# Reordering the first two slots of an eight-graph GNN and attention pipeline: mask tiles, row copies, value loads, VectorE's queue, and the last gathers ahead of a scatter

## The chip, the core and the metric

One core of a Trainium2 chip runs the whole program. The metric is the device time of one execution in microseconds; lower is better. The engines are TensorE (PE; its weight loads are PEld), VectorE (DVE), ScalarE (ACT), GpSimd (POOL) and the DMA queues, two of which are filled by SyncE (SP) and by ACT, and one by POOL.

## What is computed

The input is `x` (8 graphs, 1024 nodes, 128 features, float32) and `adj` (8 x 1024 x 1024, int32, about 8 ones in a row). Two layers follow each other, each `x = x + layer(relu(layernorm(x)))`:

```python
# layer 0: for each node, the elementwise maximum over its first 25 neighbours
agg = max(h[idx[:25]]);  out = relu(concat([h, agg]) @ W + b)
# layer 1: masked attention (8 heads of 16), then a feed-forward block
allowed = (adj > 0) | (adj.T > 0) | eye
ctx = softmax(where(allowed, q @ k.T * scale, -inf)) @ v
x = layernorm(x + ctx @ Wo.T + bo)
x = layernorm(x + relu(x @ W1.T + b1) @ W2.T + b2)
```

## The kernel before

The graphs go through a software pipeline of **slots** `s`. In slot `s` the attention of graph `g = s` runs in 32 steps `n` (a step is 8 matmuls and 16 mask matmuls of scores on PE, two exponentials on ACT, and 8 context matmuls on PE, one step behind). Around them, spread over fixed steps, run the closing work of graph `p = s-1` (output projection, feed-forward), the front of `f = s+1` (layer 0's linear part, projections, value rows, masks), the pooling of `r = s+2` and the neighbour lists of `l = s+3`. Every engine's queue is an order written out by hand, and engines meet through semaphores. An instruction that waits holds up all that stands behind it in its queue.

What the change and the prediction touch:

- **Neighbour lists** (DVE). `list_tile(l, t)` makes keys of an adjacency tile that SP loaded, and takes chunk maxima; `merge_pair` merges two tiles; `find_crowded`, `crowded_tiles`, `make_lists` and `list_ranks` finish the lists of a graph. PE helps at two steps (`RANK_AT`): it turns `full` at slot 1's step 11 for graph 3, and counts ranks at step 12 (`rank_counts`), after `make_lists` has written `abovesum`. `rank_counts` and the turn of `full` share PSUM bank 2 with `context_rows`, so they wait for `context` on DVE, which frees it.
- **Scatter and load of lists** (POOL). `scatter_lists(r)` writes the lists sorted by length to DRAM with eight indirect DMAs; `load_lists(r)` reads them back when all eight have landed; the gathers of graph `r` wait for that.
- **Gathers** (POOL). `gather_tile(f, t)` issues one indirect DMA for each neighbour level: for graphs from 2 on some 20 for tile 0, and down to 5 for tile 7. Each is held back until a step of the scores is done (`paced`, tables `PACE_2`, `PACE_3`), and the first of a tile until the tile two before it is pooled. `pool_tile(f, t)` on DVE takes the maxima, and `send(f, t)` on POOL scatters its result to DRAM. When all eight have landed SP loads them back as `ag` (`load_pooled`), and PE turns `ag` at step 20 of graph `f`'s slot `s = f-1`.
- **Order of POOL for graph 2.** Gathers of tile 6, `send(2, 4)`, `scatter_lists(3)`, `beta2(1)` (an elementwise add on 128 x 1024), gathers of tile 7, `send(2, 5)`, `load_lists(3)`, `send(2, 6)`, `send(2, 7)`, gathers of graph 3.
- **Feed-forward of graph 0, second half, in slot 1.** PE needs `add_input(0, 1)` of DVE before it can turn the sum at step 17.
- **Slot 2's step 3.** PE turns both halves of graph 1's context there, and the second half needs `context(1, 3)`, which stands behind `pool_tile(3, 3)` in DVE's queue (`middle`).
- **Masks** (ACT). `mask_tile` converts an adjacency tile and then issues the load of the next one into the same buffer `adj_m`, at the steps of `MASK_AT`.
- **Row copies** (ACT). `first_norm(l, t)` normalizes the rows of graph `l` in place at the steps of `H_AT_1` for graph 3; SP then stores them.
- **Value loads** (SP). `turn_values(f, hg)` moves the value rows of four heads with seven DMAs; the first contexts of a slot wait for `turn_values(f, 0)`. For graph 1 it stands behind `load_list_tile(3, 5)`.

Of the kernel before, what the change touches and what calls it, by code (L numbers as in the profile page):

```python
# [42 lines left out]
PACE_1 = [(4, 3, 0, 8), (9, 3, 0, 10), (11, 3, 0, 12), (13, 3, 0, 14), (14, 3, 0, 15), (15, 3, 0, 16), (16, 3, 0, 16), (16, 3, 0, 16)]  # L43
PACE_2 = [(25, 3, 0, 31), (32, 3, 1, 35), (35, 3, 1, 38), (38, 3, 1, 41), (41, 3, 1, 43), (43, 3, 1, 45), (45, 3, 2, 47), (49, 3, 0, 50)]
PACE_3 = [(19, 4, 0, 24), (24, 4, 0, 26), (27, 4, 0, 29), (29, 3, 0, 31), (32, 3, 0, 34), (35, 3, 1, 37), (38, 3, 0, 39), (43, 3, 2, 45)]
EARLY_FIRSTS = 28
SCATTER_PACE = {2: 20, 3: 47}
SCATTER_LATE = 40
# [16 lines left out]
H_AT = {17: (0, 2), 19: (2, 4), 21: (4, 5), 22: (5, 8)}  # L65
H_AT_1 = {22: (0, 4), 23: (4, 8)}

CTXT_AT, EARLY_CTXT_AT = [{3}, {3}], {20}
# [9 lines left out]
PROJ_BANK = dict(pair for pairs in PROJ_AT.values() for pair in pairs)  # L78
VALUE_BANK = (1, 2)
MASK_AT = {4: 0, 7: 1, 11: 2, 12: 3, 15: 4, 16: 5, 18: 6, 21: 7}  # L80
AGGS = 4
# [97 lines left out]
def program(nc, x, adj, L0_W, L0_b, Wqkv, bqkv, Wo, bo, ln1_g, ln1_b, W1, b1, W2, b2, ln2_g, ln2_b, out):  # L179
# [6 lines left out]
    with ctx:  # L186
# [256 lines left out]
        with nc.Block() as block:  # L443

            @block.sync
            def _(sp):
# [92 lines left out]
                def first_slot():  # L539
                    load_shift(0, 0)  # L540
                    turn_values(0, 1)
                    load_list_tile(2, 2)
                    load_list_tile(2, 3)
                    store_h_rows(2)
                    load_list_tile(2, 4)
                    load_h(1)
                    load_list_tile(2, 5)
                    load_x1_half(1, 0)
                    load_list_tile(2, 6)
                    load_x1_half(1, 1)  # L550
                    load_list_tile(2, 7)
                    load_x(3)
                    load_list_tile(3, 0)
                    load_list_tile(3, 1)
                    load_pooled(1)
                    load_shift(0, 1)
                    store_h_rows(3)
                    for t in range(2, 6):
                        load_list_tile(3, t)
                    turn_values(1, 0)  # L560

                prologue()
# [55 lines left out]
            def _(pool):  # L618
# [33 lines left out]

                def scatter_lists(r):
                    pool.wait_ge(s_ranks, 2 * (r + 1))
                    k = r % 2
                    for t in range(T):
                        pool.wait_ge(s_scores, scatter_paced(r, t))
# [58 lines left out]
                for f in range(B):  # L716
# [6 lines left out]
                    for t in range(T):  # L723
# [3 lines left out]
                        if f and t >= 2:  # L727
                            send(f, t - 2)
                        if t == T - 2 and f >= AHEAD:
                            if f + 1 < B:  # L730
                                scatter_lists(f + 1)
                            beta2(f - 1)
                    if f == 1:
                        send(f, T - 2)
                        send(f, T - 1)
                        scatter_lists(f + 1)
                        beta2(f - 1)
                    if f:
                        if f + 1 < B:
# [4 lines left out]
                            load_lists(f + 1)  # L744
                        if f >= AHEAD:
                            send(f, T - 2)
# [6 lines left out]
            def _(dve):  # L753
# [486 lines left out]
                def second_slot():  # L1240
# [12 lines left out]
                    find_crowded()  # L1253
                    merge_pair(6)
                    pool_tile(2, 3)
                    context(1, 0)
                    crowded_tiles(3)
                    make_lists(3)
                    pool_tile(2, 4)
                    list_ranks(3)  # L1260
                    list_tile(4, 0)
                    add_input(0, 0)
                    first_norm(4)
                    finish(0, 0)
                    pool_tile(2, 5)
                    list_tile(4, 1)
                    merge_pair(0)
                    wide_maxima(1, 1)
                    pool_tile(2, 6)
                    add_input(0, 1)  # L1270
                    list_tile(4, 2)
                    finish(0, 1)
                    context(1, 1)
                    pool_tile(2, 7)
                    list_tile(4, 3)
                    merge_pair(2)
# [55 lines left out]
                for s in range(1, B + 1):  # L1332
# [15 lines left out]
                    if live(r):  # L1348
                        pool_tile(r, 0)
                        pool_tile(r, 1)  # L1350
                    if live(g):
# [16 lines left out]
                    if live(f):  # L1368
                        largest(f, 3)
                        products(f)  # L1370
                        flag(f)
                    if live(r):
                        pool_tile(r, 2)
# [5 lines left out]
            def _(act):  # L1379
# [118 lines left out]
                for s in range(-3, B + 1):  # L1498
                    g, p, f, r, l = s, s - 1, s + 1, s + 2, s + 3
                    for n in range(STEPS):  # L1500
# [19 lines left out]
                        if s == -2 and n == 10:  # L1520
                            for kt, bank in NEAR_0:
                                bar(0, kt, bank, 0, s_near_counts, s_near_ready)
                        if f and live(f) and n in MASK_AT:
                            mask_tile(f, MASK_AT[n])
                        if s == 0 and n in (7, 8):
                            for t in range((n - 7) * TH, (n - 6) * TH):
                                first_norm(2, t)
                        if live(l) and l not in (0, 2):
                            for t in range(*(H_AT if l > 4 else H_AT_1).get(n, (0, 0))):
                                first_norm(l, t)  # L1530
# [385 lines left out]
```

## Time and profile before

| what | value |
|---|---|
| median of three runs | 1263.07 us (1261.59 to 1265.48) |
| the profiled execution's own time | 1266.34 us |
| its span, first to last instruction | 1263.8 us |
| PE busy, share of the span | 1053.1 us, 83% |
| ACT busy | 806.7 us, 64% |
| DVE busy | 798.5 us, 63% |
| POOL busy | 737.2 us, 58% |
| mean granted share of the TensorE clock | 0.952 |

The profile is one execution. Busy times are those of the engines, without their sequencers' waits and register work; a gap of POOL of about 0.3 us between two indirect DMAs is its issue. In a timeline the bracket tells how long the engine had been idle before the instruction, and what ended that. Engine totals say little here, since each slot has its own limits: the views by slot and by engine do.

### The profile page before, as it was taken

The numbers are of one execution on the slowest core, as the hardware profiler recorded it, in microseconds if no ns is written. First come the engines' busy times: TensorE is split into PE (matmuls) and PEld (weight loads), VectorE is DVE, ScalarE is ACT, GpSimd is POOL, SyncE is SP. The second block draws the span as 40 slices with busy tenths as digits, with TensorE's granted clock in tenths as the row PEclk, the third lists the DMA queues.
The fourth block names the chain that finished last, engine by engine and source line by source line (L and its number), as shares of the span: only waits on it lengthen the run. The fifth ranks groups of instructions, "written<-read, shape, count | busy, mean of one in ns | idle before, by whom it ended". The sixth has DMA issues, their size and how long they took to land.

```text
span 1263.8 us, 29316 instructions
## 1 busy us (share of the span) xinstructions
PE 1053.1 (83%) x11014; PEld 407.3 (32%) x11014; DVE 798.5 (63%) x3052; ACT 806.7 (64%) x1031; POOL 737.2 (58%) x743
## 2 busy tenths in 40 slices
PE   0125687788994989999999999999999999999874
PEld 0112331233331424343434333433343334333222
DVE  7856777668778476977697768776363534122323
ACT  1130256667763767788768876887778767875541
POOL 4776677557777777777777767777777620000000
PEclk9986788999997999999999999999999999999996
DMA  6743337616443535563557354623452331000000
GB/s 189 254 127 104 94 115 192 214 52 152 135 152 110 158 88 164 160 163 87 162 165 161 87 162 149 175 83 98 129 118 67 93 103 51 18 4 10 10 9 9
DMA packets 104372, 144.33 MB, mean 114 GB/s; under 512 B 18104, under 2 KB 76992, under 8 KB 104192
## 3 DMA queue, kind: packets, MB, share of 16 engines
q1 hardware_dynamic: 68352, 62.67, 16.1%
q0 software_dynamic: 22816, 44.61, 15.6%
q10 hardware_dynamic: 13024, 34.75, 8.2%
q8 instruction: 101, 1.65, 0.5%
q14 instruction: 79, 0.65, 0.2%
HBM read 124.65 MB, written 12.85 MB: 109 GB/s over the span
## 4 chain that ended last, share of the span: by engine, by line
PE 60%; ACT 13%; DVE 9%; POOL 6%; DMA 6%; issue 5%; ACTq 0%; SPq 0%; DVEq 0%; POOLq 0%
PE sc L1658 19%; PE cb L1678 12%; ACT probs L1443 11%; PE sc L1662 6%; PE m L1735 4%; PE m L1743 3%; POOL nb_low L707 3%; DMA adj_m<-in_adj_dram 3%; POOL nb_low L685 2%; PE m L1564 2%; PE sc L1700 2%; PE m L1587 2%; DMA nb_low<-h_rows,lsorted 1%; ACT m L1459 1%; PE m L1592 1%
## 5 line engine op out<-in xcount | busy, mean ns | idle before, releaser
L1443 ACT ACTIVATE probs<-sc 128x1024 f32<-128x1024 f32 x512 | 496.5, 1023 | 237.7 <-PE sc L1662 230.4
L685 POOL DMA_INDIRECT nb_low<-h_rows,lsorted x474 | 470.3, 992 | 175.4 <-issue 127.5
L1678 PE MATMUL cb<-probs,va 128*17 128x512 f32 x2048 | 272.9, 605 | 4.9 <-issue 3.9
L1658 PE MATMUL sc<-q_near,k_g 32*128 32x512 f32 x1024 | 150.4, 658 | 24.3 <-ACT probs L1443 20.5
L1658 PE MATMUL sc<-q_far,k_g 32*128 32x512 f32 x1024 | 148.7, 648 | 22.3 <-ACT probs L1443 21.2
L998 DVE TENSOR_REDUCE agg<-nb_low 128x128 f32<-128x1024 f32 (+10 forms) x58 | 96.3, 1661 | 59.4 <-DMA nb_low<-h_rows,lsorted 32.6
L1662 PE MATMUL sc<-barred,negident 32*32 32x512 bf16 x4096 | 113.2, 389 | 1.5 <-issue 1.4
L817 DVE MAX8 cand<-keys 128x8 f16<-128x128 f16 x512 | 105.3, 278 | 2.2
L707 POOL DMA_INDIRECT nb_low<-h_rows,first_lists x80 | 81.6, 1020 | 41.6 <-issue 22.9
L1662 PEld LDWEIGHTS sc<-barred,negident 32*32 32x32 bf16 x4096 | 35.4, 88 | 201.0 <-issue 201.0
L1459 ACT ACTIVATE m<-adj_m 128x1024 bf16<-128x1024 int32 x64 | 67.8, 1059 | 44.6 <-DMA adj_m<-in_adj_dram 44.6
L813 DVE SCALAR_TENSOR_TENSOR keys<-adj_t,prio 128x1024 f16<-128x1024 int32 x64 | 78.6, 1228 | 9.2 <-DVEq L1005 6.6
L1435 ACT ACTIVATE barred<-m 128x512 bf16<-128x512 f32 x128 | 72.9, 609 | 10.3 <-PE m L1592 9.4
L665 POOL DMA_INDIRECT pooled_rows<-agg,lsorted x56 | 59.4, 1060 | 27.3 <-issue 14.0
L658 POOL DMA_INDIRECT neighbour_lists<-lst,rank_i x48 | 49.4, 1028 | 31.7 <-DVE rank_i L893 18.3
L1735 PE MATMUL m<-turned,w1T 128*128 128x512 f32 x128 | 65.5, 636 | 1.0 <-ACT turned L1427 1.0
L1658 PEld LDWEIGHTS sc<-q_near,k_g 32*128 32x128 f32 x1024 | 41.1, 187 | 74.4 <-ACT probs L1443 48.3
L1658 PEld LDWEIGHTS sc<-q_far,k_g 32*128 32x128 f32 x1024 | 40.6, 184 | 70.9 <-ACT probs L1443 49.9
L1743 PE MATMUL m<-wide_tiles,w2T 128*128 128x512 f32 x128 | 63.1, 617 | 0.0
L1678 PEld LDWEIGHTS cb<-probs,va 128*17 128x17 f32 x2048 | 34.1, 95 | 64.0 <-issue 63.3
L685 POOL DMA_INDIRECT nb_high<-h_rows,lsorted x46 | 46.3, 1006 | 14.0 <-issue 12.5
L1475 ACT ACTIVATE wide_tiles<-m,b1c 128x512 f32<-128x512 f32 x64 | 44.0, 687 | 15.3 <-PE m L1735 13.8
(183 smaller groups left out, 1448.9 us busy)
## 6 DMA issues: line engine op xcount, KB each, us to landing
adj_t<-in_adj_dram SPq DMA_DIRECT2D x64, 512.0 KB
adj_m<-in_adj_dram ACTq DMA_DIRECT2D x64, 512.0 KB
nb_low<-h_rows,lsorted POOLq DMA_INDIRECT x474
xh<-in_x_dram SPq DMA_DIRECT2D x8, 512.0 KB
h_rows<-xh SPq DMA_DIRECT2D x8, 512.0 KB
hl<-h_rows SPq DMA_DIRECT2D x8, 512.0 KB
x<-in_x_dram SPq DMA_DIRECT2D x16, 256.0 KB
out_dram<-h2T SPq DMA_DIRECT2D x16, 256.0 KB
```

Source lines behind the costliest of these rows:

```text
L685: pool.indirect_dma_start(out=dst, out_offset=None, in_=h_rows[0:(f + 1) * (N + 1), :], in_offset=bass.IndirectOffsetOnAxis(ap=lsorted[:, ...
L707: pool.indirect_dma_start(out=first_slots(t)[:, k, :], out_offset=None, in_=h_rows[0:(f + 1) * (N + 1), :], in_offset=bass.IndirectOffsetO ...
L813: nc.vector.scalar_tensor_tensor(out=keys[:, t, :], in0=adj_t[:, t % 2, :], scalar=0.0, in1=prio[:, :], op0=ALU.not_equal, op1=ALU.mult).t ...
L817: ch.step(nc.vector.max(cand[:, t, 8 * c:8 * c + 8], keys[:, t, c * CW:(c + 1) * CW]))
L998: ch.link(nc.vector.tensor_reduce(a, first.rearrange("p k c -> p c k"), AX.X, ALU.max))
L1443: nc.scalar.activation(probs[:, i % 2, 2 * pair:2 * pair + 2, :], sc[:, 2 * pair:2 * pair + 2, :], ACT.Exp, scale=SCALE).then_inc(s_probs, 1)
L1459: nc.scalar.activation(m1[:, t, :], adj_m[:, :], ACT.Relu).then_inc(s_m1_ready, 1)
L1658: nc.tensor.matmul(sc[:, a, :], k[part, :], q[part, :], start=True, stop=False)
L1662: last = nc.tensor.matmul(sc[c * SPAN:(c + 1) * SPAN, a, :], negident[b, b], barred[b, kt, qh * HALF:(qh + 1) * HALF], start=False, stop=True)
L1678: last = nc.tensor.matmul(cb[a * SPAN:a * SPAN + VW, :], va[:, u % 2, a, kt, :], probs[:, i % 2, a, :], start=(kt == 0), stop=(kt == T - 1))
L1735: nc.tensor.matmul(m[:, bank, :], w1T[:, k * P:(k + 1) * P], turned[:, half * HALF:(half + 1) * HALF], start=True, stop=True).then_inc(s_h ...
L1743: last = nc.tensor.matmul(m[:, half, :], w2T[:, k, :], hid[:, k, :], start=(k == 0), stop=(k == FC - 1))
```

## The change

- `MASK_AT_0` gives the mask tiles of graph 1 (in slot 0) other steps: 4, 6, 10, 12, 14, 16, 19, 21 in place of 4, 7, 11, 12, 15, 16, 18, 21.
- `H_AT_3` moves the row copies of graph 3 from steps 22 and 23 to 24 and 25.
- On SP, `turn_values(1, 0)` goes ahead of `load_list_tile(3, 5)`.
- DVE's `second_slot` gets another order: `context(1, 0)` ahead of `pool_tile(2, 3)`; after `list_ranks(3)` come `add_input(0, 0)`, `pool_tile(2, 5)`, `list_tile(4, 0)`, `finish(0, 0)`, `first_norm(4)`, `pool_tile(2, 6)`, `wide_maxima(1, 1)`, `add_input(0, 1)`, `list_tile(4, 1)`, `finish(0, 1)`, `context(1, 1)`, `pool_tile(2, 7)`, and only then `merge_pair(0)` and the further list tiles. `pool_tile(3, 1)` moves behind `flag(2)`.
- On POOL, graph 2's gathers of tile 7 and `send(2, 5)` go ahead of the scatter of graph 3's lists. The scatter is cut in two: four tiles, `send(2, 6)`, `send(2, 7)`, four tiles, then `beta2(1)` and `load_lists(3)`.
- `PACE_2`, `PACE_3` and `SCATTER_PACE` get other steps for these parts.

```diff
--- before.py
+++ after.py
@@ -41,10 +41,10 @@
 
 PACE = [(15, 3, 0, 21), (21, 3, 1, 24), (25, 3, 0, 28), (28, 3, 2, 31), (32, 3, 0, 34), (35, 3, 1, 37), (38, 3, 0, 39), (43, 3, 2, 45)]
 PACE_1 = [(4, 3, 0, 8), (9, 3, 0, 10), (11, 3, 0, 12), (13, 3, 0, 14), (14, 3, 0, 15), (15, 3, 0, 16), (16, 3, 0, 16), (16, 3, 0, 16)]
-PACE_2 = [(25, 3, 0, 31), (32, 3, 1, 35), (35, 3, 1, 38), (38, 3, 1, 41), (41, 3, 1, 43), (43, 3, 1, 45), (45, 3, 2, 47), (49, 3, 0, 50)]
-PACE_3 = [(19, 4, 0, 24), (24, 4, 0, 26), (27, 4, 0, 29), (29, 3, 0, 31), (32, 3, 0, 34), (35, 3, 1, 37), (38, 3, 0, 39), (43, 3, 2, 45)]
+PACE_2 = [(25, 3, 0, 31), (32, 3, 1, 35), (35, 3, 1, 38), (38, 3, 1, 41), (41, 3, 1, 43), (43, 3, 1, 45), (45, 3, 2, 47), (47, 3, 1, 48)]
+PACE_3 = [(20, 4, 0, 25), (25, 4, 1, 27), (27, 4, 0, 29), (29, 3, 0, 31), (32, 3, 0, 34), (35, 3, 1, 37), (38, 3, 0, 39), (43, 3, 2, 45)]
 EARLY_FIRSTS = 28
-SCATTER_PACE = {2: 20, 3: 47}
+SCATTER_PACE = {2: 20, 3: 48}
 SCATTER_LATE = 40
 
 
@@ -64,6 +64,7 @@
 NEAR_AT_1 = {17: [(0, 2), (1, 0)], 20: [(2, 2)], 21: [(3, 2)], 23: [(4, 2)], 24: [(5, 2)], 25: [(6, 2)], 31: [(7, 2)]}
 H_AT = {17: (0, 2), 19: (2, 4), 21: (4, 5), 22: (5, 8)}
 H_AT_1 = {22: (0, 4), 23: (4, 8)}
+H_AT_3 = {24: (0, 4), 25: (4, 8)}
 
 CTXT_AT, EARLY_CTXT_AT = [{3}, {3}], {20}
 OUTPROJ_AT, EARLY_OUTPROJ_AT = [{4}, {5}], {21}
@@ -77,6 +78,7 @@
 PROJ_AT_1 = {28: [(0, 0), (1, 1)], 29: [(2, 2), (3, 0)]}
 PROJ_BANK = dict(pair for pairs in PROJ_AT.values() for pair in pairs)
 VALUE_BANK = (1, 2)
+MASK_AT_0 = {4: 0, 6: 1, 10: 2, 12: 3, 14: 4, 16: 5, 19: 6, 21: 7}
 MASK_AT = {4: 0, 7: 1, 11: 2, 12: 3, 15: 4, 16: 5, 18: 6, 21: 7}
 AGGS = 4
 
@@ -555,9 +557,10 @@
                     load_pooled(1)
                     load_shift(0, 1)
                     store_h_rows(3)
-                    for t in range(2, 6):
+                    for t in range(2, 5):
                         load_list_tile(3, t)
                     turn_values(1, 0)
+                    load_list_tile(3, 5)
 
                 prologue()
                 first_slot()
@@ -650,10 +653,10 @@
                     k = r % 2
                     pool.dma_start(lsorted[:, k, :, :], rows_of(lists[k])).then_inc(s_lists_in, 16)
 
-                def scatter_lists(r):
+                def scatter_lists(r, tiles=(0, T)):
                     pool.wait_ge(s_ranks, 2 * (r + 1))
                     k = r % 2
-                    for t in range(T):
+                    for t in range(*tiles):
                         pool.wait_ge(s_scores, scatter_paced(r, t))
                         pool.indirect_dma_start(out=lists[k][:, :], out_offset=bass.IndirectOffsetOnAxis(ap=rank_i[:, t:t + 1], axis=0),
                                                 in_=lst[:, t, :], in_offset=None).then_inc(s_lists_out, 16)
@@ -726,7 +729,7 @@
                         gather_tile(f, t)
                         if f and t >= 2:
                             send(f, t - 2)
-                        if t == T - 2 and f >= AHEAD:
+                        if t == T - 2 and f > AHEAD:
                             if f + 1 < B:
                                 scatter_lists(f + 1)
                             beta2(f - 1)
@@ -735,6 +738,12 @@
                         send(f, T - 1)
                         scatter_lists(f + 1)
                         beta2(f - 1)
+                    if f == AHEAD:
+                        scatter_lists(f + 1, (0, TH))
+                        send(f, T - 2)
+                        send(f, T - 1)
+                        scatter_lists(f + 1, (TH, T))
+                        beta2(f - 1)
                     if f:
                         if f + 1 < B:
                             if f == 1:
@@ -742,7 +751,7 @@
                             for k in range(AGGS) if f > 1 else ():
                                 pool.wait_ge(s_pooled_out[k], 16 * T // AGGS * (f - 1))
                             load_lists(f + 1)
-                        if f >= AHEAD:
+                        if f > AHEAD:
                             send(f, T - 2)
                             send(f, T - 1)
                 beta2(B - 1)
@@ -1252,26 +1261,26 @@
                     list_tile(3, 7)
                     find_crowded()
                     merge_pair(6)
+                    context(1, 0)
                     pool_tile(2, 3)
-                    context(1, 0)
                     crowded_tiles(3)
                     make_lists(3)
                     pool_tile(2, 4)
                     list_ranks(3)
+                    add_input(0, 0)
+                    pool_tile(2, 5)
                     list_tile(4, 0)
-                    add_input(0, 0)
+                    finish(0, 0)
                     first_norm(4)
-                    finish(0, 0)
-                    pool_tile(2, 5)
+                    pool_tile(2, 6)
+                    wide_maxima(1, 1)
+                    add_input(0, 1)
                     list_tile(4, 1)
-                    merge_pair(0)
-                    wide_maxima(1, 1)
-                    pool_tile(2, 6)
-                    add_input(0, 1)
-                    list_tile(4, 2)
                     finish(0, 1)
                     context(1, 1)
                     pool_tile(2, 7)
+                    merge_pair(0)
+                    list_tile(4, 2)
                     list_tile(4, 3)
                     merge_pair(2)
 
@@ -1347,7 +1356,8 @@
                         low_levels(r)
                     if live(r):
                         pool_tile(r, 0)
-                        pool_tile(r, 1)
+                        if s > 1:
+                            pool_tile(r, 1)
                     if live(g):
                         context(g, 2)
                     if s == B - 1:
@@ -1369,6 +1379,8 @@
                         largest(f, 3)
                         products(f)
                         flag(f)
+                    if s == 1:
+                        pool_tile(r, 1)
                     if live(r):
                         pool_tile(r, 2)
                     if live(l):
@@ -1520,13 +1532,14 @@
                         if s == -2 and n == 10:
                             for kt, bank in NEAR_0:
                                 bar(0, kt, bank, 0, s_near_counts, s_near_ready)
-                        if f and live(f) and n in MASK_AT:
-                            mask_tile(f, MASK_AT[n])
+                        masks = MASK_AT_0 if f == 1 else MASK_AT
+                        if f and live(f) and n in masks:
+                            mask_tile(f, masks[n])
                         if s == 0 and n in (7, 8):
                             for t in range((n - 7) * TH, (n - 6) * TH):
                                 first_norm(2, t)
                         if live(l) and l not in (0, 2):
-                            for t in range(*(H_AT if l > 4 else H_AT_1).get(n, (0, 0))):
+                            for t in range(*(H_AT if l > 4 else H_AT_3 if l == 3 else H_AT_1).get(n, (0, 0))):
                                 first_norm(l, t)
                         if live(f):
                             if n in (18, 19) if f else n in (3, 4):
```

## Rows read from the trace of the kernel before

**Rows 1.** Windows of slots 0 to 2: length, then busy us of PE, PEld, DVE, ACT, POOL.

```profile
166.40:303.40 137.00, 113.33 (x1382) 41.56 (x1386) 100.50 (x420) 94.92 (x124) 89.25 (x87) 0.95 0.50 143
303.40:466.00 162.60, 130.76 (x1355) 49.77 (x1347) 119.21 (x435) 100.26 (x129) 124.26 (x122) 0.92 0.47 132
466.00:592.50 126.50, 124.00 (x1360) 47.87 (x1363) 95.75 (x363) 100.19 (x129) 96.00 (x96) 1.00 0.51 143
```

**Rows 2.** Timeline of ACT, slot 0: start, us, instruction [idle before <-releaser].

```profile
221.18 1.06 ACT L1459 ACTIVATE m<-adj_m 128x1024 bf16<-128x1024 int32 x1 [3.87 <-DMA adj_m<-in_adj_dram]
...
238.88 1.06 ACT L1459 ACTIVATE m<-adj_m 128x1024 bf16<-128x1024 int32 x1 [1.95 <-DMA adj_m<-in_adj_dram]
...
264.56 1.65 ACT L1467 ACTIVATE xh<-xh,nw 128x128 f32<-128x128 f32 x4 [3.68 <-DVE nw L781]
```

**Rows 3.** Timeline of PE, slot 1.

```profile
310.49 1.91 PE L1678 MATMUL cb<-probs,va 128*17 128x512 f32 x8 [3.88 <-issue]
...
354.84 0.27 PE L1839 MATMUL m<-identf,full 128*1 128x128 f32 x1 [1.59 <-DVE ctxn L1017]
...
390.84 1.11 PE L1751 MATMUL m<-identf,turned 128*128 128x128 f32 x4 [9.52 <-DVE turned L1037]
```

**Rows 4.** Timeline of POOL, slots 0 and 1.

```profile
258.25 1.17 POOL L658 DMA_INDIRECT neighbour_lists<-lst,rank_i  x1 [11.15 <-DVE rank_i L893]
...
366.66 0.94 POOL L685 DMA_INDIRECT nb_low<-h_rows,lsorted  x1 [0.30 <-PE sc L1662]
...
378.03 1.23 POOL L658 DMA_INDIRECT neighbour_lists<-lst,rank_i  x1 [0.30 <-issue]
...
389.08 2.35 POOL L714 TENSOR_TENSOR x<-x,bias_rows 128x1024 f32<-128x1024 f32 x1
...
404.09 1.88 POOL L665 DMA_INDIRECT pooled_rows<-agg,lsorted  x1 [1.93 <-DMA lsorted<-neighbour_lists]
...
406.28 1.00 POOL L685 DMA_INDIRECT nb_low<-h_rows,lsorted  x1 [0.31 <-issue]
```

**Rows 5.** Chain of work of slot 1, in order of time: start, us, what.

```profile
356.58 3.03 DMA nb_low<-h_rows,lsorted
...
399.70 4.19 DMA lsorted<-neighbour_lists
...
404.09 3.15 DMA pooled_rows<-agg,lsorted
...
407.39 4.23 DMA ag<-pooled_rows
```

**Rows 6.** Timeline of DVE, slot 1 and the start of slot 2.

```profile
363.07 1.22 DVE L813 SCALAR_TENSOR_TENSOR keys<-adj_t,prio 128x1024 f16<-128x1024 int32 x1
...
366.54 1.64 DVE L758 BATCH_NORM_STATS2 st<-xh 128x6 f32<-128x128 f32 x8
...
371.54 0.88 DVE L758 BATCH_NORM_STATS2 st<-m 128x6 f32<-128x128 f32 x4
...
378.42 1.73 DVE L998 TENSOR_REDUCE agg<-nb_low 128x128 f32<-128x896 f32 x1
...
388.11 1.46 DVE L998 TENSOR_REDUCE agg<-nb_low 128x128 f32<-128x768 f32 x1 [2.25 <-issue]
...
390.04 0.75 DVE L1037 SCALAR_TENSOR_TENSOR turned<-m,b2c,turned 128x512 f32<-128x512 f32 x1 [0.46 <-DVEq L1005]
...
394.12 0.87 DVE L758 BATCH_NORM_STATS2 st<-m 128x6 f32<-128x128 f32 x4
...
402.17 1.29 DVE L998 TENSOR_REDUCE agg<-nb_low 128x128 f32<-128x640 f32 x1 [0.28 <-issue]
...
471.19 2.16 DVE L998 TENSOR_REDUCE agg<-nb_low 128x128 f32<-128x1152 f32 x1 [2.75 <-DMA nb_low<-h_rows,lsorted]
...
474.10 0.42 DVE L1017 TENSOR_TENSOR ctxn<-m,rden 128x256 f32<-128x256 f32 x1
```

**Rows 7.** Timeline of PE, fourth step of slot 2.

```profile
477.64 1.09 PE L1564 MATMUL m<-identf,ctxn 128*128 128x128 f32 x8
```

## The prediction

> **What bounds the kernel now.** I first read the windows by slot [rows 1]. Slot 2 takes 126.5 us with PE busy for 124.0 at the full clock: a settled slot is PE's. Slots 0 and 1 take 137.0 and 162.6 us, so there are some 10 and 36 us above a settled slot, and all that this change can give lies there. The same rows show the second bound. POOL has 96 instructions in slot 2, nearly all indirect DMAs of 0.94 us with a gap of 0.30 [rows 1, 4]: 96 x 1.25 = 120 of 126.5 us. In slot 1 it is 122 instructions, 122 x 1.25 = 152 of 162.6. So GpSimd, which the page lists at 58%, has 6 us of room in a settled slot, and whatever makes its queue late stays late for slots.
>
> Next I read the timelines of the waits. In slot 0 ACT waits twice for the one mask buffer, 3.87 and 1.95 us, and once, 3.68 us, for the rows of graph 3 [rows 2]. In slot 1 PE waits 3.88 us at the first contexts, 1.59 us for `context(1, 0)`, and 9.52 us for `add_input(0, 1)` [rows 3]. At step 20 it waits again: lists load, send, load of `ag` in a chain of 4.19, 3.15 and 4.23 us [rows 5].
>
> **The change part by part.**
>
> *Masks.* With two steps between a load and its use both mask waits can go: up to 3.87 + 1.95 = 5.8 us. *Row copies*: up to 3.68 us, less what the four copies (1.65 us, [rows 2]) add to each of two later steps. I take 2. *Value loads*: seven DMAs start earlier and without an adjacency tile of 512 KB ahead of them; the 3.88 us go. The tile's own load is then some seven issues later, and `list_tile(3, 5)` stands behind two other large parts of DVE's queue, so that cover hides it. *context(1, 0)*: 1.59 us.
>
> None of this reaches the end by itself, since in slot 1 the next thing late is the pooling of graph 2, and that is POOL's. How much earlier does POOL get? Its graph 2 work begins with the scatter, which waited 11.15 us for the ranks [rows 4], a product of DVE and PE. The mask waits lie ahead of it, so POOL gains between 0 and 5.8 us; DVE is busy for 100.5 of 137 us there [rows 1] and would be next. I take 2.5.
>
> *DVE's second slot.* Before, tile 5 of graph 2 was pooled late enough (378.42, no wait) [rows 6]. Its last gather is issued at 366.66 [rows 4], and a gather lands 3.0 us after its issue [rows 5], so the data is there at 369.7, or 367.2 with POOL 2.5 earlier. In the new order only `add_input(0, 0)` stands between `list_ranks(3)` (its end is 363.07, with the shift 360.6) and this pooling: DVE now idles some 6 us, which is as much as it saves by moving a list tile and a merge back. From 367.2 on the queue runs without waits [rows 6]:
>
> - `pool_tile(2, 5)` 1.73 + 0.46 = 2.2
> - `list_tile(4, 0)`: 366.54 - 363.07 = 3.5 with `add_input` in it, less its 0.75 = 2.7
> - `finish(0, 0)`: 378.42 - 371.54 = 6.9
> - `first_norm(4)`: 371.54 - 366.54 = 5.0
> - `pool_tile(2, 6)` 1.46 + 0.46 = 1.9, and the value load of `wide_maxima`, at most the 2.25 seen before 388.11
>
> Sum 21.0: `add_input(0, 1)` starts at 388.2 in place of 390.04. PE's long wait is hardly shorter: 1.8 us gained. Then `add_input` and a list tile 3.5, `finish(0, 1)` and `context(1, 1)` 402.17 - 394.12 = 8.1, `pool_tile(2, 7)` 1.3: it is done at 401.1, where it was 403.5.
>
> *POOL's order.* Before, scatter (378.03 to 389.08, 11.05 us for eight) and `beta2` (2.35) ran while DVE was on its way to tile 7, and the lists' load landed just before the last send; the first gather of graph 3 came at 406.28 [rows 4]. Now half of the scatter, `beta2` and the load stand behind `send(2, 7)`, which waits for 401.1. POOL has nothing to do while it waits there. After it: send 1.3, four scatters 5.5, `beta2` 2.5, load until landed 4.2 [rows 5], and 0.2: the first gather of graph 3 comes at 401.2 + 13.7 = 414.9, which is **8.6 us later** than before. With POOL's gain at its bounds (0 and 5.8) it is 11.1 or 5.3 later.
>
> The Trainium skill ("DMA: Bandwidth & Descriptors", section "Anatomy of one DMA - SWDGE (gpsimd) path") has 2.0 us plus the bytes over 436 GB/s for a DMA that GpSimd issues, 2.3 us for the 128 KB of lists. The row shows 4.19, and the measurement decides; by the page's figure the delay would be 1.9 us less and the forecast 1267.
>
> *Where it lands.* In the rest of slot 1 the new place of `pool_tile(3, 1)` frees `context(1, 2)` from a late gather, and `ag` comes at 401.2 + 3.15 + 4.23, some 3 us earlier than before, if no list tile's load gets ahead of it. Slot 2 can thus start up to 4 us early. But at slot 2's step 3 PE needs `context(1, 3)`, which stands behind `pool_tile(3, 3)`, and that one already waited 2.75 us for its gathers and started at 471.19 [rows 6]. Between there and 406.28 POOL ran back to back, so it moves by the full 8.6: to 479.8. The context was done at 474.5, 3.3 us after 471.19 [rows 6]; now 483.1. PE wanted the first half at 477.64 and the second about 0.5 later [rows 7], so there was a slack of 3.6, and PE is 8.6 - 3.6 = 5.0 us later than before. After such an idle stretch eight context matmuls take 1.91 us [rows 3], and slot 1's clock is 0.92 against 1.00 in slot 2 [rows 1]; that, and the next pooled tiles that are 8.6 late too, add between 0 and 3.6 (then nothing of the slack is left). I take 1. From there slots are PE's again and don't give it back; POOL's 6 us of room per slot only restores its slack.
>
> **Sum.** +6.0 us. The profiled execution took 1266.34, so 1272.3 in its terms; it lies 3.3 above the median of the runs, so the median goes from 1263.07 to 1269.1. With the bounds of the delay: 5.3 - 3.6 = +1.7, and 11.1 - 3.6 + 1.5 = +9: own range 1264.8 to 1272.
>
> **The rivals.**
>
> *A. The delay doesn't reach PE.* If the first gather of graph 3 starts before 406.28 + 3.6 = 409.9, slot 2 keeps its early start and the kernel is 4 us faster, 1259. It needs `pool_tile(2, 7)` done by 396.1, 5 us ahead of my sum, so POOL's gain at its bound and a shorter queue on DVE. For: the list tile and the merge are out of the way. Against: the 34 us behind tile 5 are plain durations. 0.15.
>
> *B. Most waits come out in full*: 5.8 + 3.7 + 3.9 + 1.6 = 15.0 us, 1248. For: each is on PE's or ACT's own queue. Against: POOL fills 152 us of slot 1. The Trainium skill ("Perfetto Trace Analysis", section "Optimization Strategies") speaks for this one: when TensorE idles for another engine, speed up what blocks it. 0.07.
>
> *C. The two cancel*: the delay is 3 to 6 us, most of it slack, and the time stays within 0.3%. 0.20.
>
> **Chances.** Forecast 0.58, A 0.15, B 0.07, C 0.20. A change within 0.3%, 3.8 us, can't be told from none. Faster 0.22 (A, B), same 0.20, slower 0.58. The range leaves B out and takes A's time in with 2 us about it, and 1 us above my own range: 1257 to 1273.
>
> **What the next profile would show.** Right: ACT's two mask waits and the wait before the first contexts are gone; DVE idle before `pool_tile(2, 5)`, about 6 us; PE's wait at step 17 still over 8 us; POOL idle about 10 us ahead of `send(2, 7)`; the first gather of graph 3 at 413 to 417; slot 2's fourth step with a PE wait of 8 to 9 us for `context(1, 3)`. Wrong: if that first gather comes by 410, A holds; if slot 2 has no such wait though the gather is late, DVE's slack was larger than rows 7 tell; if tile 5 lands before 364, all times of DVE after it move, and the forecast with them.

## The result and the profile after

The kernel after takes **1274.66 us** (median of four runs, 1273.75 to 1275.99) where the kernel before takes 1262.33 (four runs beside it). The ratio is 1.0097, with a 95% interval of 1.0081 to 1.0113: **12.3 us slower**. The sign was forecast; the size was put at +6.0, and 1274.66 lies above the range (1257 to 1273). The profiled execution of the kernel after took 1275.99 us, 9.65 more than the profiled one of before (1266.34). The first lies 1.3 us above the median of its kernel's runs and the second 4.0, so the traces show a smaller difference than the medians do.

The starts of the steps on PE, read from the two timelines and subtracted, say where the time went. Slot 0 starts 2.2 us earlier, slot 1 3.6 earlier and slot 2 0.2 earlier; the two steps behind the turn of graph 1's context in slot 2 start 10.1 and 11.1 *later*, and from there the distance stays between 11.4 and 10.2 to the end. So all of the loss that the traces show is one stall. The windows of slots 0 to 2 (columns as in [rows 1]) show it in the third row, with 10.9 us more than before for the same work:

```profile
164.20:299.50 135.30, 109.79 (x1382) 41.27 (x1386) 100.23 (x417) 94.55 (x124) 88.13 (x84) 0.94 0.49 142
299.50:465.60 166.10, 132.41 (x1354) 49.74 (x1348) 113.91 (x428) 101.03 (x129) 114.00 (x114) 0.92 0.46 128
465.60:603.00 137.40, 125.47 (x1340) 48.26 (x1340) 97.21 (x372) 100.20 (x128) 105.38 (x105) 0.96 0.48 136
```

The timeline of PE has the stall itself, the turn of the second half of graph 1's context in slot 2's fourth step, and ahead of it the wait at step 17 of slot 1:

```profile
389.58 1.12 PE L1764 MATMUL m<-identf,turned 128*128 128x128 f32 x4 [9.29 <-DVE turned L1046]
...
487.63 1.12 PE L1577 MATMUL m<-identf,ctxn 128*128 128x128 f32 x4 [9.55 <-DVE ctxn L1026]
```

The timeline of DVE: tile 5 of graph 2, the second half's `add_input`, tile 7, and then tiles 2 and 3 of graph 3 with the context that PE waits for:

```profile
367.67 1.71 DVE L1007 TENSOR_REDUCE agg<-nb_low 128x128 f32<-128x896 f32 x1 [5.08 <-DMA nb_low<-h_rows,lsorted]
...
388.77 0.75 DVE L1046 SCALAR_TENSOR_TENSOR turned<-m,b2c,turned 128x512 f32<-128x512 f32 x1 [1.97 <-issue]
...
400.02 1.26 DVE L1007 TENSOR_REDUCE agg<-nb_low 128x128 f32<-128x640 f32 x1 [0.28 <-issue]
...
470.50 2.39 DVE L1007 TENSOR_REDUCE agg<-nb_low 128x128 f32<-128x1280 f32 x1 [7.71 <-DMA nb_low<-h_rows,lsorted]
484.33 2.08 DVE L1007 TENSOR_REDUCE agg<-nb_low 128x128 f32<-128x1152 f32 x1 [5.75 <-DMA nb_low<-h_rows,lsorted]
487.15 0.42 DVE L1026 TENSOR_TENSOR ctxn<-m,rden 128x256 f32<-128x256 f32 x1
```

And the timeline of POOL: the first scatter in slot 0, and then from the last send of graph 2 to the first gather of graph 3:

```profile
257.50 1.17 POOL L661 DMA_INDIRECT neighbour_lists<-lst,rank_i  x1 [10.61 <-DVE rank_i L902]
...
401.92 0.97 POOL L668 DMA_INDIRECT pooled_rows<-agg,lsorted  x1 [11.84 <-DVEq L1016]
403.19 0.97 POOL L661 DMA_INDIRECT neighbour_lists<-lst,rank_i  x1 [0.30 <-issue]
...
408.97 2.35 POOL L717 TENSOR_TENSOR x<-x,bias_rows 128x1024 f32<-128x1024 f32 x1
413.87 0.93 POOL L654 DMA_DIRECT2D lsorted<-neighbour_lists  x1 [2.55 <-issue]
419.15 1.01 POOL L688 DMA_INDIRECT nb_low<-h_rows,lsorted  x1 [4.34 <-issue]
```

Read from the last list back to the first, this is the whole delay. The first gather of graph 3 starts at 419.15 against 406.28 [rows 4], 12.9 us later. Tile 3 is pooled at 484.33 against 471.19 [rows 6], 13.1 later. PE had 3.6 us of slack there and waits 9.55.

### The profile page after: what moved, and what is told of

It is laid out like the page before. It is cut to its first block, busy times and chain, and to the rows that moved or that the text cites. A ratio compares the mean times of both kernels' runs of the same rounds, so it can differ in the third digit from the quotient of the medians.

```text
span 1274.1 us, 29318 instructions
## 1 busy us (share of the span) xinstructions
PE 1054.0 (83%) x11014; PEld 408.3 (32%) x11014; DVE 795.0 (62%) x3052; ACT 807.8 (63%) x1031; POOL 731.9 (57%) x743
## 4 chain that ended last, share of the span: by engine, by line
PE 59%; DVE 12%; ACT 12%; DMA 6%; POOL 5%; issue 5%; DVEq 0%; ACTq 0%; POOLq 0%; SPq 0%
PE sc L1671 18%; PE cb L1691 11%; ACT probs L1455 10%; PE sc L1675 6%; PE m L1748 4%; PE m L1756 3%; POOL nb_low L710 3%; DMA nb_low<-h_rows,lsorted 3%; PE m L1577 3%; POOL nb_low L688 2%; DVE agg L1007 2%; PE m L1600 2%; PE sc L1713 2%; PE m L1605 1%; PE m L1778 1%
```

## The experiments

All ratios are to the kernel before on the same chip, with 95% intervals; before took 1263.1 to 1263.2 us beside e1 to e9, and 1262.55 beside e14 to e17. "Landed" is the start of `pool_tile(3, 3)`, which waits for tile 3's gathers (before: 471.19; after: 484.33), and "PE's wait" is the one at slot 2's fourth step. The landed times hold to some 3 us only: e1 and e8, whose code is the same up to there, start slot 1 4.0 and 6.9 us earlier than before does. A wait is read within one execution and is free of that.

| run | what | us | ratio | landed | PE's wait |
|---|---|---|---|---|---|
| e1 | after, old order on POOL | 1265.88 | 1.0032 (1.0015 to 1.0050) | 475.6 | 6.69 |
| e2 | before, new order and pace tables of POOL | 1275.18 | 1.0090 (1.0066 to 1.0114) | 489.2 | 18.13, elsewhere |
| e3 | after, both sends last | 1268.71 | 1.0052 (1.0026 to 1.0078) | 476.2 | 6.63 |
| e7 | after, scatter and `beta2` in the gap | 1268.91 | 1.0046 (1.0030 to 1.0062) | 479.0 | 7.65 |
| e8 | e1 with old `PACE_3` | 1266.73 | 1.0033 (1.0016 to 1.0050) | 472.9 | 7.04 |
| e9 | e8, loads held | 1264.36 | 1.0016 (0.9996 to 1.0036) | 473.7 | 3.47 |
| e4 | before, slot 0's edits | 1261.32 | 0.9988 (0.9973 to 1.0002) | 465.7 | under 1 |
| e5 | before, DVE's orders | 1270.40 | 1.0052 (1.0029 to 1.0074) | 477.5 | 6.60 |
| e14 | before, `pool_tile(3, 1)` late | 1266.11 | 1.0030 (1.0012 to 1.0047) | 476.7 | 7.53 |
| e15 | after, `pool_tile(3, 1)` back | 1275.56 | 1.0112 (1.0089 to 1.0136) | 483.2 | 15.31, elsewhere |
| e16 | e9, `pool_tile(3, 1)` earlier | 1262.12 | 0.9998 (0.9983 to 1.0013) | 469.7 | under 1 |
| e17 | e4 with e16's last two edits | 1261.06 | 0.9991 (0.9976 to 1.0007) | 471.3 | 1.12 |

### Is it the order on POOL?

**e1** is the kernel after with before's queue on POOL; **e2** is the kernel before with after's queue on POOL. Cut of e1's edit, against the kernel after:

```diff
-                    if f == AHEAD:
-                        scatter_lists(f + 1, (0, TH))
-                        send(f, T - 2)
-                        send(f, T - 1)
-                        scatter_lists(f + 1, (TH, T))
-                        beta2(f - 1)
```

> The changed kernel with GpSimd's old order for graph 2 (whole scatter and beta2 ahead of the gathers of tile 7, lists' load ahead of the last two sends, old PACE_2 and SCATTER_PACE). Theory (GpSimd's lists come late): the first gather of graph 3 is back at 403 to 407 us and the wait at slot 2's step 3 is gone, 1258 to 1262 us. Rival (VectorE's new order, with pool_tile(2,5) and pool_tile(3,1) elsewhere, makes slot 2 late): still 1270 to 1275.

> The kernel before with GpSimd's new order and the new pace tables alone. Theory: pool_tile(2,7) ends near 403.5, so the first gather of graph 3 comes at 419 to 422 and the time is 1275 to 1278 us. Rival (VectorE's order): within 3 us of before, 1260 to 1265.

e2 alone costs 12 us, as much as the whole change, and lies in its range; its first gather of graph 3 came later still than expected (424.50). But taking the same edit out of the whole (e1) gives back only some 8 of them: e1 is still 1.0032, where the theory had a gain over before. In e1 the first gather of graph 3 is early (403.79), and yet PE waits 6.69 us at the same place. Something else in the change makes the same data late.

**e3** and **e7** keep the new order otherwise and only move what stands behind the sends: in e3 scatter, `beta2` and load all go ahead of `send(2, 6)`, in e7 the load alone stays behind. Cut of e3's edit, against the kernel after (its two sends now follow the load):

```diff
-                        scatter_lists(f + 1, (0, TH))
+                        scatter_lists(f + 1)
+                        beta2(f - 1)
                         send(f, T - 2)
                         send(f, T - 1)
-                        scatter_lists(f + 1, (TH, T))
-                        beta2(f - 1)
```

> The changed kernel, but after the gathers of tile 7 GpSimd issues all eight scatters, beta2 and the lists' load, and the two sends last. Theory: it has the early gathers without the wait ahead of the lists; first gather of graph 3 at 403 to 407, time 1258 to 1262. Rival: 1270 to 1275.

> The changed kernel with all eight scatters and beta2 ahead of the two sends, the lists' load behind them. Only the load (some 5.3 us from issue to landing) stands behind the wait for pool_tile(2,7). Theory: first gather of graph 3 near 408.5, 2 us later than before, inside VectorE's slack at slot 2's step 3: 1260 to 1263. If there is no slack and each us of delay costs one: 1264 to 1266. Rival (VectorE's order): 1270 to 1275.

Both missed in the same way as e1. The first gather came at 404.22 and 409.24, 14.9 and 9.9 us earlier than after, yet the time fell by about 6 us, not 12. They size the queue behind `send(2, 7)`: with nothing there (e3) the first gather follows 1.3 us after it, with the load alone (e7) 5.4 us (403.88 to 409.24), with all (after) 17.2. What keeps them above before looks like what e1 has: big loads of SP at 466.67 and 468.38, and a last gather of tile 3 that takes 6.88 and 6.42 us.

### What else makes tile 3 late?

Windows of 468 to 476 us, of the kernel before and then of e1 (the last three columns are PE's granted clock, the DMA engines' share and GB/s):

```profile
468.00:476.00 8.00, 7.92 (x96) 2.91 (x93) 3.64 (x8) 6.40 (x10) 6.12 (x7) 1.00 0.60 164
```

```profile
468.00:476.00 8.00, 4.24 (x51) 1.70 (x47) 0.36 (x1) 4.53 (x7) 6.13 (x7) 1.00 0.91 294
```

The queue of SP (SPq is its sequencer), before and then in e1, says what those 294 GB/s are:

```profile
472.37 1.06 SPq L452 DMA_DIRECT2D adj_t<-in_adj_dram  x2
```

```profile
465.90 1.06 SPq L454 DMA_DIRECT2D adj_t<-in_adj_dram  x2
```

with graph 5's `x` and graph 3's `hl` right behind, some 2 MB. Before, they are issued at 472.4, just after tile 3 of graph 3 has landed (it is pooled from 471.19 on). In e1 slot 2 starts 6.8 us earlier, SP gets to them at 465.9, and tile 3's gathers, issued from 458.70 to 469.65, land among them. In the chain of waits the last gather takes 6.84 us, where the one of the kernel after takes 3.56, and before it was some 3.1 (issued at 468.05, pooled from 471.19 on):

```profile
468.70 6.84 DMA nb_low<-h_rows,lsorted
```

The other cause is on POOL in e1: waits for `PACE_3` of 1.24 and 0.88 us, and 1.04 for `pool_tile(3, 1)`. **e8** puts `PACE_3` back, and **e9** adds a wait on SP, so that the loads can't come ahead of tile 3. The edit of e9 that e8 lacks:

```diff
+                    if s == 2:
+                        sp.wait_ge(s_pooled, T * f + 4)
                     # then adj(5, 0), adj(5, 1), x(5), h(3)
```

> e1_pool_order_back with the old PACE_3 too. In e1 GpSimd waited 1.24 and 0.88 us for steps 22 and 24 of the scores between gathers of graph 3. Theory: tile 3 of graph 3 lands some 2 us earlier than in e1, and the time is 2 us less, 1263 to 1265. Rival (the gathers' landing is set by the big loads alone): as e1, 1265 to 1267.

> e8_old_pace3, and in slot 2 SyncE holds the loads of graph 5's first two adjacency tiles, its rows and graph 3's rows (2 MB) until pool_tile(3,3) is done. In e1 they were issued at 466 to 468 us, ahead of the last gathers of tile 3, which landed 5.9 us after their end instead of 2.1. Theory (slot 2 starts early, so these loads collide with the gathers that it waits for): landing within 3 us of the last gather's end, and the time 3 to 4 us below e8: 1259 to 1261.5. Rival (the lateness is VectorE's order and GpSimd's queue): as e8, 1263 to 1266.

e8 brought nothing by itself, as its rival had it. The two waits of pace are gone, but POOL now stands 2.28 us ahead of tile 3's gathers, and the last gather takes 7.24 us. e9 shows the collision's price. In e8 the loads are issued 2.8 us ahead of the last gather (462.77, 465.58), in e9 6.3 us behind it (476.19, 469.90): it takes 3.71 us, PE waits 3.47 in place of 7.04, and the time is 1264.36. That misses the 1259 to 1261.5 of the theory, and can't be told from before, nor by these intervals from e8; what is shown is the shorter wait. What is left in e9 is a gap of POOL that `pool_tile(3, 1)` ends (its buffer is the one that tile 3's gathers fill):

```profile
459.64 0.97 POOL L690 DMA_INDIRECT nb_low<-h_rows,lsorted  x1 [3.68 <-DVEq L1012]
```

### One part at a time

**e4** has masks, row copies and value loads alone, **e5** DVE's `second_slot` and the late `pool_tile(3, 1)`, and **e14** only the latter. The edit of e14, against the kernel before, cut:

```diff
                         pool_tile(r, 0)
-                        pool_tile(r, 1)
+                        if s > 1:
+                            pool_tile(r, 1)
...
                         flag(f)
+                    if s == 1:
+                        pool_tile(r, 1)
```

> The kernel before with the three edits of slot 0 alone (mask steps, row copies, value loads ahead of one adjacency tile). Theory: slot 1 starts 4 us earlier, but graph 2's pooling in slot 1 is GpSimd's, so the time is within 2 us of before, 1261 to 1264. Rival (waits of slot 0 come out in full): 1255 to 1259. Rival (these edits are what costs in e1): 1265 to 1267.

> The kernel before with VectorE's new orders alone. pool_tile(3,1) behind flag(2) lets slot 2 start early and holds the gathers of tile 3 by about 1 us. Theory (slot 2's loads then collide with the gathers of tile 3): 1265 to 1268. Rival (the order is what it gains by): 1258 to 1261.

> The kernel before with one edit: pool_tile(3,1) is issued behind flag(2) instead of behind sweep 2's first step. Theory (its later end holds GpSimd some 2 to 4 us ahead of tile 3's gathers of graph 3, and the gathers then land among the loads of slot 2): 1266 to 1270 us, with a GpSimd gap of over 2 us that ends on VectorE just before tile 3's gathers. Rival (the gap fits in the slack of 3.6 us that context(1,3) had): within 2 us of the kernel before, 1261 to 1265 us.

e4 is at most a small gain (0.9973 to 1.0002), as expected. e5 (slower than its 1265 to 1268) and e14 (in its range) are both slower with the same picture: POOL's gap ahead of tile 3 (3.67 and 2.27 us), big loads early (467.89 and 466.27), last gather 6.55 and 7.24 us. The timeline of POOL and the chain, in e14:

```profile
458.99 0.97 POOL L685 DMA_INDIRECT nb_low<-h_rows,lsorted  x1 [2.27 <-DVEq L1007]
```

```profile
469.32 7.24 DMA nb_low<-h_rows,lsorted
```

So one moved line costs 3.6 us, though slot 2 starts 6.5 us *earlier* by it: the later pooling frees `context(1, 2)`, PE turns to slot 2 sooner, SP's loads come sooner, and tile 3 is 5.5 us later for both reasons (its last gather is issued 1.3 us later and takes some 4.1 longer).

**e15** asks whether that adds to POOL's new order. It is the kernel after with `pool_tile(3, 1)` at its old place:

> The kernel after with pool_tile(3,1) back at its old place. Theory (GpSimd is late anyway by its own new order, so the place of pool_tile(3,1) costs nothing more here): 1273 to 1276 us, no different from the kernel after. Rival (the two delays add): 1267 to 1270 us.

It doesn't: 1275.56 (1.0112) against 1274.66 (1.0097). POOL is late anyway, and the stall only changes its place, to slot 1's second-last steps, where PE waits for `context(1, 2)` behind the now early `pool_tile(3, 1)`:

```profile
460.33 1.08 PE L1804 MATMUL m<-h2T,wqk 128*32 128x512 f32 x6 [15.31 <-DVE ctxn L1026]
```

That is also what e2's 18.13 us are. Two causes that make the same data late overlap: alone they cost 12 us (e2) and 7 us (e5), together 12.

### Is there something to win?

**e16** is the kernel after without its three delays: old order on POOL with old `PACE_3`, the loads held as in e9, and `pool_tile(3, 1)` between `largest(2, 1)` and `merge_pair(4)`. **e17** has the last two on top of e4, so DVE's second slot is as before. The move of `pool_tile(3, 1)` in both, against the kernel before, cut:

```diff
                         pool_tile(r, 0)
-                        pool_tile(r, 1)
+                        if s > 1:
+                            pool_tile(r, 1)
...                      # behind largest(f, 1)
+                    if s == 1:
+                        pool_tile(r, 1)
```

> The kernel after with the old order on GpSimd, pool_tile(3,1) between largest(2,1) and merge_pair(4), and SyncE's loads of graph 5's adjacency and features held until pool_tile(3,3). Theory (what made the change slow was GpSimd's order, the late pool_tile(3,1), and the early big loads; with all three gone the new slots 0 and 1 keep their gain): 1256 to 1261 us, TensorE waits under 2 us at the fourth step of slot 2. Rival (TensorE's order sets the time whatever is gained in the first slots): 1262 to 1265 us.

> The kernel before with slot 0's edits alone (mask tiles, row copies, value loads), pool_tile(3,1) between largest(2,1) and merge_pair(4), and the loads of graph 5 held until pool_tile(3,3). Theory: 1257 to 1262 us; if it is as fast as e16_both_removed, VectorE's new order of the second slot brings nothing. Rival (the new order of the second slot carries the gain): 1261 to 1264 us, with e16_both_removed at least 2 us faster.

The stall is gone in both. Slot 2's fourth step, timeline of PE in e16:

```profile
472.93 1.09 PE L1573 MATMUL m<-identf,ctxn 128*128 128x128 f32 x8
```

Yet 1262.12 (0.9998) and 1261.06 (0.9991) can't be told from before. e16 missed its 1256 to 1261 and came where its rival had it. e17 lies where theory and rival overlap, but the rival also wanted e16 2 us faster, which it isn't: DVE's new second slot brings nothing that these runs show. In e16's trace PE's steps lie 3 to 5 us ahead of before's from there on, but before's traced execution is itself 4.0 us above its median. Four of these kernels were also run in an earlier group, on a chip where the kernel before itself took 1476.51 us and PE waited at other places, so only ratios can be read there. e10 is the same kernel as e16, e11 as e17, e12 as e15 and e13 as e14:

> e9_loads_held with pool_tile(3,1) between largest(2,1) and merge_pair(4), where its gathers have landed and nothing of PE waits for it. Theory: GpSimd's wait of 3.7 us before tile 3 goes, tile 3 lands 3 to 4 us earlier, and so does slot 2's step 3: 1258.5 to 1261.5. Rival (the rest of VectorE's second slot is late too): as e9, 1263 to 1265.

> e4_slot0_edits (VectorE's and GpSimd's old orders) with pool_tile(3,1) between largest(2,1) and merge_pair(4), and slot 2's loads held as in e9. Theory: context(1,2) no longer waits for tile 1, so slot 2 starts some 3 us earlier than in e4, and the gathers of tile 3 are neither held nor met by the loads: 1 to 3 us below e4, 1258 to 1260.5. Rival (slot 2's step 3 is as early as graph 3's gathers allow): as e4, 1261 to 1262.

> The changed kernel with pool_tile(3,1) back at its old place behind pool_tile(3,0). There GpSimd's queue is so late that it never waited for tile 1's buffer (no gap over 0.31 us among the gathers). Theory (the two delays don't add, since they cover each other): no gain, 1273 to 1278, or somewhat slower, since context(1,2) stands behind the late gathers of tile 1 again. Rival (each edit costs its own 5 to 7 us): 1267 to 1270.

> The kernel before with one edit: pool_tile(3,1) behind flag(2). In the runs with GpSimd's old order and this place, its queue stood 2.3 to 3.7 us before the gathers of tile 3 of graph 3, which wait for tile 1's buffer. Theory: that wait appears here too, slot 2 starts about 3 to 5 us early, its big loads meet the gathers of tile 3, and the time is 4 to 7 us above before, 1267 to 1270. Rival (the second slot's order, ahead of it, is what costs in e5): within 2 us of before.

In this order they were 0.9942 (0.9919 to 0.9966), 0.9977 (0.9953 to 1.0000), 1.0074 (1.0041 to 1.0107) and 1.0052 (1.0026 to 1.0078). The losses show on both chips; e10's gain doesn't (the same kernel as e16, 0.9998). Whether this arrangement is a better one stays open; where the kernel runs at its usual speed it is worth at most 2.2 us (0.9983).

## Why the prediction was right in the place and wrong in the size

**The mechanism and the place.** *Where it lands* named the first gather of graph 3, then `pool_tile(3, 3)`, `context(1, 3)` and PE at slot 2's fourth step, and this is where the 11 us are. e2 has the price of POOL's order alone, though its stall is elsewhere. Rivals A, B and C are out by the time. A is out as a mechanism too: in e1, e3 and e7 the first gather of graph 3 starts by 409.9, as A wants it, and they are slower than before; and e16, with nothing late, is not 4 us faster either (0.9983 to 1.0013).

**Steps that held.** `pool_tile(2, 5)` at 367.67 (367.2 said) after an idle stretch of 5.1 (6 said); `add_input(0, 1)` at 388.77 (388.2); PE's wait at step 17 was 9.29 (over 8); POOL idle 11.84 ahead of `send(2, 7)` (10); `pool_tile(2, 7)` done at 401.3 (401.1). The slack of 3.6 held to 0.1: tile 3 is 13.1 us late, less 3.6 is 9.5, and PE waits 9.55. The mask waits went from 5.8 us to 0.3, the row copies' wait went, and PE's wait at the first contexts fell from 3.88 to 1.16. e4 bounds what all of slot 0's edits are worth at 3.4 us (0.9973), where their waits sum to 13.4 (15.0 less the 1.6 of `context(1, 0)`), so that little of them reaches the end, as said. POOL's gain of 2.5 was 2.2 where the forecast uses it (tile 5's last gather is issued at 364.43 against 366.66), but only 0.75 at the scatter that the working started from. In slot 0 PE, now earlier, waits 10.09 us for `full`, which `find_crowded` writes on DVE:

```profile
246.24 0.37 PE L1852 MATMUL m<-identf,full 128*1 128x128 f32 x1 [10.09 <-DVE full L851]
```

**One reading was off without harm.** The chain of [rows 5] runs from the lists' load to the send, and the working took it as a wait. In the code `send(2, 7)` waits for `pool_tile(2, 7)`, which ends at 403.46, not for the load, and in e14's trace the same gap (1.94 us) is put down to DVE.

**The step that failed** is the sum "After it: send 1.3, four scatters 5.5, `beta2` 2.5, load until landed 4.2 [rows 5], and 0.2", 13.7 us in all. Measured from 401.92 to 419.15 it is 17.2: send 1.3, scatters 5.8, `beta2` 2.35, **a wait of 2.55 that the sum lacks**, the load 3.9 until it landed at 417.8, and **1.35 from there to the first gather**, where the sum has 0.2. In that last piece POOL reads the tile's count out of the lists (`value_load`); before, in slot 1, the last send stood between, and the gather followed it 0.31 us later.

The wait of 2.55 is `load_lists`' own: it needs all eight scatters landed, and the last one, issued at 407.71, landed 5.1 us later. That is not what a scatter takes by itself. The four early ones, ahead of `send(2, 6)`, landed in 2.1 to 2.5 us. In e7 the last one landed in 2.1, and in e3 `beta2` alone, 2.35 us, hid the landing, for the load is issued right behind it. What differs is the traffic. The sends let SP load `ag` (at 405.83), and adjacency tiles and more go beside it, on top of the late scatters. Windows of the kernel after and of e7, each from the last scatter's issue to its landing (the last two columns are the DMA engines' share and GB/s):

```profile
407.70:412.80 5.10, 1.92 (x11) 1.59 (x12) 5.00 (x30) 0.60 (x1) 3.58 (x2) 0.50 1.08 339
```

```profile
392.80:394.90 2.10, 2.10 (x12) 0.71 (x5) 2.03 (x4) 2.10 (x3) 2.07 (x2) 0.50 0.05 10
```

So by these traces the wait is a collision with bulk loads again; no run held those loads back, so that cause is argued and not shown. Before, in slot 1, the gathers of tile 7 and `send(2, 5)` stood between scatter and load as well, so [rows 4, 5] show no such wait. But the trace of before holds the same sequence of instructions a slot earlier, for graph 2. Timeline of POOL, kernel before:

```profile
263.55 0.97 POOL L658 DMA_INDIRECT neighbour_lists<-lst,rank_i  x1 [0.30 <-issue]
...
268.36 2.37 POOL L714 TENSOR_TENSOR x<-x,bias_rows 128x1024 f32<-128x1024 f32 x1
272.20 0.95 POOL L651 DMA_DIRECT2D lsorted<-neighbour_lists  x1 [1.46 <-issue]
277.27 1.01 POOL L685 DMA_INDIRECT nb_low<-h_rows,lsorted  x1 [4.12 <-issue]
```

From the fifth scatter to the first gather are 13.7 us, with the send 15.0, where my parts gave 13.7 with the send. Priced by it, the first gather would have come at 416.2 and the median near 1270.4. The piece behind the load's landing is there too: landed 3.6 us after 272.20, gather 1.5 later. Its wait of 1.46, though, seems to have another cause, which no view names. In slot 0 of the kernel after POOL idles 2.34 us at the same place, though the last two scatters landed 2.7 to 3.0 us after their issue, before `beta2` ended. So of the two pieces that the look-up adds, some 1.5 us each, the wait would have been luck. The other 3.0 us to 419.15 are 0.7 of a later start, 1.0 in the four scatters (5.8 for 4.8; two issues took 1.67 and 1.23), 1.1 in the wait (2.55 for 1.46) and 0.2 in load and gather. The sign in *What the next profile would show*, 413 to 417, was missed with them. The 2.3 us that the Trainium skill ("DMA: Bandwidth & Descriptors", section "Anatomy of one DMA - SWDGE (gpsimd) path") would give the load is further from the 3.9 measured to its landing than my 4.2 was.

**The term for the clock** was put at 1.0 and is 1.6 (11.1 less 9.5). After the idle stretch PE runs at a lower granted clock (third last column). Windows of the kernel after: the idle stretch, then 4 us, then 4 more:

```profile
478.00:487.60 9.60, 0.08 (x1) 0.00 (x0) 3.37 (x9) 0.98 (x2) 7.29 (x8) 0.64 0.56 168
487.60:491.60 4.00, 3.97 (x33) 1.61 (x37) 1.48 (x7) 0.80 (x2) 3.09 (x4) 0.58 0.19 51
491.60:495.60 4.00, 4.00 (x51) 2.03 (x47) 2.10 (x8) 3.25 (x5) 3.02 (x4) 1.00 0.20 53
```

A granted share of 0.58 is mostly the lower level, 1.2 GHz; 0.42 of 4 us is 1.7, against the 1.6 measured. In sum, 5.0 + 1.0 was forecast at this place, and 9.5 + 1.6 came.

**What was not seen.** *Where it lands* let slot 2 start up to 4 us early and saw no cost in it, and rival A counts it as a gain. The runs show a cost: in e1, e8 and e14 slot 2 starts 6.5 to 10 us early, SP's loads follow PE's steps and come down on tile 3's gathers (6.8 to 7.2 us for the last one, 3.7 with the loads held). And `pool_tile(3, 1)`'s new place was read for what it frees on DVE, not for the buffer it holds on POOL. In the kernel after slot 2 starts only 0.2 us early, and both lie in the shadow of POOL's own delay (e15), so they don't change the forecast's sum. With POOL's order out of the way (e1) the kernel is at 1265.88, 3 us *above* before.

**Open.** The rest, between the 11.1 us of the traces and the 12.3 of the medians, is not located; the traced execution of before lies 4.0 above its kernel's median. What ends POOL's wait ahead of the load in slot 0 is not known. Whether slot 0's earlier steps could be made to count was not tried: the step that starts at 245.9 before starts 12.3 us earlier after, the next one only 2.3, since PE waits for `full` between them.

## What to carry to other kernels

Before a sequence is priced from its parts, look for the same sequence elsewhere in the trace: it has the pieces between the parts, though each has to be checked for the same cause. A wait for one's own DMA to land is hidden by what stands between issue and wait, and how much cover it takes depends on what else is on the DMA engines then: `beta2`'s 2.35 us were enough in e3, and in the kernel after POOL waited another 2.55. An earlier start of a stage is not free while bulk loads are paced by that stage: ask which small, urgent transfers they will meet. And when two edits delay the same data, the one that is taken back alone tells only what the other leaves uncovered; test each part alone on the old kernel as well.

## What the hardware showed

- The last gather of tile 3 took 3.6 us from issue to landing in the kernel after (DMA engines busy for 0.46 of that stretch, 147 GB/s), and 6.8 in e1 (0.91, 294 GB/s, 2 MB of bulk loads). With these loads issued 6.3 us behind it in place of 2.8 us ahead it took 3.71 in place of 7.24 (e9, e8).
- A scatter of lists landed 2.1 to 2.5 us after its issue for the first four of graph 3 in the kernel after and 2.1 for the last one in e7 (DMA share 0.05, 10 GB/s), but 5.1 for the last one in the kernel after (1.08, 339 GB/s).
- The 128 KB load of the lists landed 4.2 us after its issue before and 3.9 after, in slot 1; in slot 0 it took 3.6 and 2.9. The first gather started another 1.35 to 1.5 us later where nothing of POOL stood between.
- A chip ran the unchanged kernel at 1476.51 us (32 runs, 1469 to 1487), 17% above the others. Ratios of single edits kept their sign there when they were losses, and one did not when it was a gain.
